# A fused linear-attention and quantized feed-forward kernel: feed-forward weights rounded by ScalarE's square, other banks for their transposes, other orders in the first and the last steps

## The reference

```
q, k = relu(x @ Wq) + 0.001, relu(x @ Wk) + 0.001        # 16 heads of 64
v = x @ Wv
context = cumsum(k (x) v); D_inv = 1 / (cumsum(k) . q)
attn = (q . context) * D_inv;  return attn @ Wo + bo

def fp4_quant_dequant(x):                                # blocks of 16 on the last axis
    scale = max(max|x| / 6, 1e-12)
    q = GRID[searchsorted(MID, |x / scale|)] * sign(x) * scale      # grid 0 .5 1 1.5 2 3 4 6
fp4_linear(x, w) = quant(x) @ quant(w).T
ffn(x) = fp4_linear(silu(fp4_linear(x, w_gate)) * fp4_linear(x, w_up), w_down)
```

## Time and profile before

| | us |
|---|---|
| median of 3 runs | 1744.37 (1743.95 to 1745.25) |
| the profiled execution | 1745.42 |
| its span, first to last instruction | 1743.4 |
| TensorE busy | 1678.0 (96%) |
| VectorE, ScalarE, GpSimd busy | 1159.6, 647.5, 454.8 |
| mean granted TensorE clock | 0.984 of full |

### The profile page before, as it was taken

One profiled execution on the slowest core, in us unless ns is written; L12 is line 12 of the kernel. 1 busy time (PEld: TensorE's weight loads), 2 busy tenths in 40 slices (PEclk: granted clock), 3 DMA queues, 4 the chain that ended last, 5 costly groups with the idle time before them and its releaser, 6 DMA issues.

```text
span 1743.4 us, 47014 instructions
## 1 busy us (share of the span) xinstructions
PE 1678.0 (96%) x20388; PEld 1590.3 (91%) x20388; DVE 1159.6 (67%) x2458; ACT 647.5 (37%) x1233; POOL 454.8 (26%) x643
## 2 busy tenths in 40 slices
PE   6679999999999999999999999999999999999985
PEld 5579999999999999999999999999999999999975
DVE  7547666766666766666676666677666667666674
ACT  5133333334333334334333433334343333343321
POOL 5342222222222222222222222122222222222211
PEclk9789999999999999999999999999999999999998
DMA  3100000000000000000000000000000000000000
GB/s 141 34 2 5 14 11 14 14 14 5 14 11 14 14 14 5 14 14 11 14 14 14 5 14 11 14 14 14 5 14 14 11 14 14 14 5 14 5 8 12
DMA packets 21963, 26.27 MB, mean 15 GB/s; under 512 B 1792, under 2 KB 20736, under 8 KB 21760
## 3 DMA queue, kind: packets, MB, share of 16 engines
q1 hardware_dynamic: 21760, 23.27, 4.2%
HBM read 14.88 MB, written 8.39 MB: 13 GB/s over the span
## 4 chain that ended last, share of the span: by engine, by line
PE 92%; DVE 4%; POOL 1%; ACT 1%; issue 1%; DMA 0%; POOLq 0%; DVEq 0%
PE bank L387 62%; PE bank L483 7%; PE bank L443 7%; PE bank L507 3%; PE bank L474 3%; PE bank L546 3%; PE bank L453 3%; PE bank L497 3%; PE bank L524 1%; PE bank L397 1%; DVE probs L1022 0%; PE bank L577 0%; DVE hid L988 0%; DVE h_amax L976 0%; DVE w_magic L944 0%
## 5 line engine op out<-in xcount | busy, mean ns | idle before, releaser
L649 ACT ACTIVATE qkT<-bank 128x512 f32<-128x512 f32 x256 | 153.4, 599 | 305.8 <-PE bank L387 305.8
L821 POOL TENSOR_SCALAR qkT<-qkT 128x512 f32<-128x512 f32 x256 | 174.9, 689 | 322.7 <-ACT qkT L649 322.7
L387 PE MATMUL bank<-xT_hi,wqk_hi 128*128 128x256 f32 x1024 | 211.8, 288 | 0.2 <-DVE wu_lo L896 0.2
L387 PE MATMUL bank<-xT_lo,wqk_hi 128*128 128x256 f32 x1024 | 203.2, 279 | 0.0
L387 PE MATMUL bank<-xT_hi,wqk_lo 128*128 128x256 f32 x1024 | 203.0, 279 | 0.0
L896 DVE TENSOR_TENSOR hqT_lo<-bank,hqT_hi 128x512 fp32r<-128x512 f32 (+1 forms) x128 | 68.3, 556 | 183.2 <-ACT hqT_hi L703 183.2
L1022 DVE TENSOR_TENSOR probs<-bank,causal 128x512 f32<-128x512 f32 x256 | 163.9, 682 | 10.9 <-PE bank L443 10.5
L850 POOL TENSOR_TENSOR rstd<-var,minus_half 128x1 f32<-128x1 f32 x64 | 35.1, 549 | 510.9 <-DVE var L1073 510.9
L387 PEld LDWEIGHTS bank<-xT_hi,wqk_hi 128*128 128x128 f32 x1024 | 155.5, 188 | 2.4 <-issue 0.3
L387 PEld LDWEIGHTS bank<-xT_lo,wqk_hi 128*128 128x128 f32 x1024 | 156.4, 188 | 0.0
L387 PEld LDWEIGHTS bank<-xT_hi,wqk_lo 128*128 128x128 f32 x1024 | 156.4, 188 | 0.0
(11 more groups left out here) (151 smaller groups left out, 3708.5 us busy)
## 6 DMA issues: line engine op xcount, KB each, us to landing
x_in<-in_L_attn_x SPq DMA_DIRECT2D x32, 256.0 KB, 2.7
out<-out_sb SPq DMA_DIRECT2D x64, 128.0 KB, 1.7
probs<-in_L_attn_Wv SPq DMA_DIRECT2D x1, 1024.0 KB, 5.0
qkT<-in_L_attn_Wq SPq DMA_DIRECT2D x1, 1024.0 KB, 7.3
qkT<-in_L_attn_Wk SPq DMA_DIRECT2D x1, 1024.0 KB, 9.3
attn<-in_L_attn_Wo SPq DMA_DIRECT2D x1, 512.0 KB, 10.2
x<-in_L_attn_Wo SPq DMA_DIRECT2D x1, 512.0 KB, 11.0
hid<-in_L_ffn_w_down SPq DMA_DIRECT2D x1, 352.0 KB, 3.0
```

The source lines that it names most:

```text
L387: at = pe.matmul(dst, lhs_at(kt), rhs_at(kt), start=first and kt == 0, stop=last and kt == k_tiles - 1)
L649: act.activation(flat(qkT[:, 2 * m:2 * m + 2, :]), bank[bank_of["qk", c, n]][:], ACT.Relu).then_inc(qk_relu, 1)
L821: pool.tensor_scalar(at, at, QK_EPS, 1.0, ALU.add, ALU.mult).then_inc(qk_ready, 1)
```

## The change

1. **Rounding of the weights.** `round_magic`, the tiles `w_magic` and GpSimd's add and subtract are gone. VectorE's `quantize` becomes `quantize_begin` and `quantize_end`, with ScalarE's `square_weights` between them, as for activations. GpSimd keeps only the multiplication by the scale (`scale_weights`).
2. **Split of the attention weights.** The high part of Wv is now a VectorE copy (ahead of ScalarE's other four), and the low parts of Wo move from GpSimd to VectorE.
3. **Banks.** A job's transposes take the bank entry of a stage that does not exist yet in that step (`W_BANKS`), and the table of places starts in step 0: no job is transposed ahead of step 0.
4. **First steps.** `quantize_begin`, `quantize_end` and the squares are put at places of their own in the orders of VectorE, ScalarE and GpSimd.
5. **Last steps.** The last two steps with attention (g = 62 and 63, `last`) do the transposes of xq and hq first, the down product before attention, and scale h one step after the other. The three draining steps have an order of their own on ScalarE (`tail`) and VectorE.

```diff
+        JOBS_AT = {(0, "attend"): (0,), (0, "update"): (1,), (0, "end"): (2,), (1, "scores"): (3,),
+                   (1, "project"): (4,), (1, "end"): (5,), (2, "scores"): (6,), (2, "attend"): (7,)}
+        W_BANKS = [("hq", 0, 0), ("hq", 0, 1), ("down", 0, 0), ("xq", 1, 0), ("gate_up", 1, 0), ("down", 1, 0),
+                   ("kv", 2, 0), ("av", 2, 3), ("hq", 2, 0), ("hq", 2, 1)]
...
-                        k = banks.take(pe, ("w", "first", m), 0, ffn_w_ready, lambda b, m=m: m + 1)
+                        k = banks.take(pe, W_BANKS[m], 0, ffn_w_ready, lambda b, m=m: m + 1)
...
+                last = now and not following
...
+                if last:
+                    turn_xq(b, c, g - 2)
+                    for n in range(2):
+                        turn_hq(b, c, g - 3, n)
                 if now:
                     scores(b, c, g, u)
...
+                if last:
+                    down(b, c, g - 3)
...
+            def square_weights(job):
+                act.wait_ge(ffn_w_step, 4 * job + 4)
+                cols = ffn_jobs[job][2]
+                act.activation(w_square[:, job % 2, 0:cols], w_stage[job % 3][:, 0:cols], ACT.Square,
+                               scale=SQUARE_SCALE).then_inc(ffn_w_square, 1)
...
-                    pool.tensor_tensor(scaled, scaled, magic, ALU.add).then_inc(ffn_w_round, 1)
-                    pool.wait_ge(ffn_w_round, 2 * job + 1)
-                    pool.tensor_tensor(scaled, scaled, magic, ALU.subtract).then_inc(ffn_w_round, 1)
...
-                if exists(g - 2, ALL_CHUNKS) and (c % 2 == 1 or g >= ALL_CHUNKS):
+                if exists(g - 2, ALL_CHUNKS) and (c % 2 == 1 or g >= ALL_CHUNKS - 2):
...
+            dve.tensor_copy(hi, src).then_inc(wv_hi_ready, 1)
+            low(lo, src, hi, wv_hi_ready, 1, attn_w_ready)
             low_x("first", 0)
...
+            def quantize_end(job):
+                cols = ffn_jobs[job][2]
+                tile, square = w_stage[job % 3][:, 0:cols], w_square[:, job % 2, 0:cols]
+                dve.wait_ge(ffn_w_square, job + 1)
+                dve.scalar_tensor_tensor(tile, square, SQUARE_SHIFT, tile, ALU.add, ALU.add).then_inc(ffn_w_grid, 1)
+                dve.wait_ge(ffn_w_grid, 2 * job + 1)
+                dve.scalar_tensor_tensor(tile, square, SQUARE_SHIFT, tile, ALU.add, ALU.subtract
+                                         ).then_inc(ffn_w_grid, 1)
...
+                    elif gated:
+                        low_xq()
+                        for half in range(2):
+                            gated_by_silu(half)
+
+                        dve.wait_ge(hq_ready, g - 2)
+                        begin_h()
+                        for n in range(2):
+                            low_hq(n)
+                        round_h(g - 2)
+                        residual()
```

More of the change, by code:

```diff
@@ L610, in step @@
                         project_qk(b, c, u + 1, 2 * n, 2 * n + 2)
-                    if downed and (now or not gated):
+                    if downed and (following or not gated):
                         turn_hq(b, c, g - 3, n)
@@ L623, in step @@
                     project_qk(b, c, u + 1, 4, PAIRS)
-                if downed:
+                if downed and not last:
                     down(b, c, g - 3)
@@ L693, in step @@
                 project = c % 2 == 1 and now and following
+                if not now:
+                    tail(b, c)
+                    return
+                last = not following
                 def high_attn(n):
@@ L733, in step @@
                         relu_qk(c, u + 1, 2 * n + 1)
-                    if downed and (now or not gated):
+                    if downed and not last:
                         high_hq(n)
+                    if g == 1 and n == 1:
+                        square_weights(6)
                 high_ffn_weights(jobs_at(g, "project"))
@@ L746, in step @@
                         high_attn(half)
-                if downed and gated and not now:
-                    for n in range(2):
-                        high_hq(n)
                 if project:
@@ L998, in low_ffn_weights @@
                         m += first_turn_of(job)
-                        low(lo[:, rows, cols], part(turn[bank_of["w", "first", m]]), hi[:, rows, cols],
+                        low(lo[:, rows, cols], part(turn[bank_of[W_BANKS[m]]]), hi[:, rows, cols],
                             ffn_w_hi, m + 1, ffn_w_ready)
@@ L1004, in _ @@
             ln1_var_of(1)
-            quantize(0)
-            quantize(1)
-            quantize(2)
-            low_ffn_weights(JOBS_AT["before"])
+            for n in (3, 4):
+                src, hi, lo = attn_weights[n]
+                low(lo, src, hi, attn_w_hi, n, wo_w_ready)
+            quantize_begin(0)
+            quantize_begin(1)
+            quantize_end(0)
+            quantize_begin(2)
+            quantize_end(1)
+            quantize_end(2)
             def step(b, c):
@@ L1059, in step, with low_xq, variance @@
                 following = exists(u + 1, ALL_HALVES)
+                last = now and not following
                 norm = c % 2 == 1 and now and exists(u + 2, ALL_HALVES)
+                def low_xq():
+                    low(flat(xqT_lo[:]), flat(turn[bank_of["xq", c, 0]][:, 0:KD, :]), flat(xqT_hi[:]),
+                        xqT_hi_ready, g - 1, xqT_ready)
+                def variance():
+                    dve.bn_aggr(mv2[:], stats2[:]).then_inc(ln2_mean, 1)
+                    dve.wait_ge(ln2_mean, g)
+                    dve.tensor_scalar(minus_mean2[:], mv2[:, 0:1], -1.0, None, ALU.mult)
+                    dve.tensor_scalar(var2[:], mv2[:, 1:2], LN_EPS, None, ALU.add).then_inc(ln2_var, 1)
@@ L1102, in step @@
                     add_state()
+                if is_step(0):
+                    quantize_end(3)
+                if is_step(1):
+                    quantize_begin(6)
                 low_ffn_weights(jobs_at(g, "update"))
-                if downed and (now or not gated):
+                if downed and not last:
                     for n in range(2):
@@ L1134, in step @@
                     ln1_var_of(u + 2)
-                if gated and (c % 2 == 1 or not now):
+                if gated and (c % 2 == 1 or last):
                     round_h(g - 2)
-                if downed:
-                    dve.wait_ge(down_done, g - 2)
-                    if g >= 5:
-                        dve.wait_ge(out_stored[c % 2], 16 * ((g - 3) // 2))
-                    dve.tensor_tensor(out_sb[:, c % 2, :], bank[bank_of["down", c, 0]][:, 0:DIM],
-                                      x2[:, (c - 3) % CHUNKS, :], ALU.add).then_inc(out_ready, 1)
+                if downed and not last:
+                    residual()
                 if now:
```

288 lines of the change are left out of this document (181 added, 107 removed).

## The result

The changed kernel takes 1718.38 us (median of 4 runs, 1716.63 to 1720.26) against 1744.31 of the kernel before on the same chip (4 runs, 1743.95 to 1745.25): a ratio of 0.9851, 95% interval 0.9834 to 0.9868. That is 25.9 us less, where 31.8 were forecast. The profiled execution of it took 1718.61, with a span of 1716.2.

What follows compares the result with a forecast made beforehand. TensorE was taken as full from 160 to 1640 us, leaving only the ends: 29.1 us gained at the front plus 2.7 at the back, 31.8 off the 1743.4 span, forecast a median of 1712.6 us, range 1703 to 1723.

Steps and rivals of the forecast that it cites:

- The full stretch: 160 to 1640 us, TensorE busy 1479.85 of 1480 us at clock 1.00: the change has nothing to win there.
- First products: Start of launch: VectorE's Wv copy takes 1.2 to 2.29 us; values start at 9.15, end at 17.4 instead of 20.08.
- Weight pieces: Weight jobs at the front: chain from begin to hq ready 5.1 us instead of 6.6; VectorE ends jobs 0 to 2 at 30.0.
- the 0.7 us that I added for two meetings: Step 0, ahead of the output projection: two VectorE instructions beside GpSimd add 0.7 us, 41.8 to 42.5.
- The two waits: TensorE waits 3.5 us at step 1's state update and 3.0 for step 2's keys, plus slow clock of 1.35 and 1.3.
- Last steps: Steps 62 to the end: 0.4 us gained by step 65's gates, 2.3 at the end, 2.7 in all.
- 3.5 late in all: By step 63, hq's transposes ahead of the scores and other new waits put TensorE 3.5 us behind the old order.
- C: Rival: the 3.5 us lost by step 63 are not won back, VectorE's queue only moving waits: 1718.8 us; chance 0.14.
- B: Rival: more waiting at the front, from VectorE contending with GpSimd, step 2 and a slow clock: 1722 us; chance 0.12.
- A: Rival: VectorE is 3 us faster, so the new front waits and their slow clock (9.2 us) go: 1703.4; chance 0.14.
- D: Rival: slower, because the long stretch loses its full clock or its order's fit; chance 0.03.
- E: Rival: nothing happens, since the jobs' real limit is their loads: 1744 us; chance 0.02.

Runs made afterwards that it cites:

- wv_scalar: The changed kernel with Wv's high-part copy back on ScalarE ahead of its other copies, VectorE only subtracting: 1720.01 us.
- k_first: The changed kernel with ScalarE's copies of the transposed keys ahead of the normalization of x2 in step 2 alone: 1713.74 us.
- old_places: The changed kernel with its new rounding, but the weight jobs at the places and in the banks of the kernel before: 1731.67 us.
- drain_only: The changed kernel with steps 62 and 63 in the order of before, new orders kept for draining steps 64 and 65: 1710.73 us.

## Why the prediction was right, and where it was off

**Where the time is.** Right in the main. The full stretch bounded the kernel, and all but 2.1 us of the gain came from the 11 us wait, the slow clock behind it and the first products.

**The number.** In the spans 27.2 us were gained where 31.8 were forecast: 3.4 too few at the front, 3.3 too few at the back, and 2.1 in the middle that nobody had counted on. That the total is off by 4.6 and not by 6.7 is luck.

**First products.** The copy took 1.23 us, near its lower bound of 1.2, so the values started at 9.22 and did not wait. (The Trainium skill, VectorE: DVE Perf Modes, "Mode 2×_2P", says that a float32 copy within SBUF makes two results a cycle; the trace agrees, 1.23 for 2048 columns against 2.29 for the subtraction.) The projections ended at 27.9 instead of 28.7. How much of these 3 us reaches the end of the sum, wv_scalar leaves open, between 1.6 and 4.

**Weight pieces.** The step that failed at the front is "products that lay beside GpSimd's work ... mostly lie alone", with the 0.7 us that I added for two meetings. VectorE ended jobs 0 to 2 at 32.3, not 30.0: up to there six instructions stood behind GpSimd's, for 0.30, 0.41, 0.74, 0.41, 0.41 and 0.96 us, 3.2 in all, and later 0.74 at 41.76, 0.37 at 53.39, 0.87 at 70.30 and 1.07 at 81.39. The last of these also held the low part of job 5, which the key transposes of step 2 waited for.

**Steps 0 to 2.** Output projection of step 0 ended 46.8 (forecast 45.35), state update of step 1 began 60.5 (59.05), that of step 2 97.3 (93.9). The two waits have the causes that were forecast and nearly the sizes, and k_first confirms the second, slow clock included. Of the 3.4 us that are missing, 1.45 are there by the end of step 0, ahead of both waits, where the meetings of the last paragraph lie. The other 1.9 arise between the two state updates: a wait of 0.58 at 73.64 for a low part of w_up, behind the meeting at 70.30; 0.5 in the wait for k_tok; and the price of the slow clock, put at 1.35 and 1.3. By the windows it was 1.7 each time (0.73, 0.50 and 0.91 in the 2 us windows from 60 to 66; 0.56 and 0.59 from 88 to 92). No run took the meetings away, so their share is argued from the timelines.

**Last steps.** The forecast gain of 2.7 is not there, and by its own sign, a back longer than before, the prediction was wrong here. "3.5 late in all" by the end of step 63 was 6.2; the draining steps' 6.2 were 5.6 in this execution, and up to 7.8 in others with the same orders. The single waits were well forecast (3.87 for 3.65, 1.48 for 1.35, 1.12 for 1.15). What failed is that the sum priced no slow clock behind 5.4 us of idle time in step 63 (and took off about 0.5 for the one of before), although it did so for every wait at the front: the scores alone lost 1.73 us, the down product behind them about 0.5. The wait of 2.27 at the gate of step 65 was not seen at all; I had the residual put ahead of h's rounding and did not ask what stood behind the rounding. The last scaling came 5.9 us behind the last product, as forecast.

**The full stretch.** "The change has nothing to win there" was wrong by 2.1 us, for a reason that no view of the profile of before could show.

**What made the gain.** Of 25.9 us the places make 13 to 16 (old_places), the banks nothing, the Wv copy 1.6 to 4, where the tiles lie 1.8 to 2.5, the last steps nothing. The rest, some 3 to 10, falls to the shorter rounding with Wo's move; that is by subtraction and was not run alone. The prediction did not separate places from banks.

**Rivals.** C (the last steps cost) gave 1718.8, and 1718.4 was measured, but that is chance. It had a loss of 3.5 us and no gain behind it, because VectorE's queue only moves the waits; there were a loss of 6.2 and a gain of 5.6, and drain_only shows that the waits are not just moved. B's contention is what happened at the front. A, D and E did not occur.

## What to carry to other kernels

Do not move work that must wait ahead of work that is free to run: the new order of steps 62 and 63, with hq's transposes ahead of the scores, cost 6 to 8 us, and the waits of 3.71, 3.47 and 3.87 us in the changed kernel were each paid a second time in the slow clock behind them. Where two in-order engines hold each other up, put the instructions that meet apart, and count a meeting as the rest of the other's instruction, not as a factor. When an edit has several halves, measure them apart: here the sum of zero hid one half worth 8 us and another that cost as much.

## What the runs showed of the hardware

**VectorE beside GpSimd is a stop, not a slow-down.** In the changed kernel's trace 30 of the 66 small instructions that make h_scale (0.186 us alone, one source, in SBUF) start while a GpSimd instruction runs; all of these take the rest of GpSimd's plus their own 0.186 less 0.146 to 0.148. GpSimd stands likewise: its scaling at 80.58, which began beside VectorE's rounding at 80.42, took 2.02 us, the next one of the same size at 89.44 took 1.39. Not touched are reductions (0.68 at 25.15, beside a GpSimd instruction), reciprocals (0.35 at 26.82, likewise) and subtractions with a source in PSUM (0.68 at 43.11, beside the addition at 42.60). Nor was a subtraction of two sources in SBUF at 18.11 beside GpSimd's power over two columns; that power, begun at 17.15 beside the subtraction before it, itself took 1.61 where it took 0.71 at 5.11. The Trainium skill (SBUF — State Buffer, "Who interferes with whom") says it of one shared pair of ports: an exclusive lock, which whoever starts first keeps for the whole instruction. Apart from 18.11 the trace agrees. I had priced a meeting by one row of before (1.28 for 0.69), 0.59; it can be the whole of GpSimd's instruction.

**Where tiles lie in SBUF moved TensorE's pace** by 0.07 us in 30.56, as shown above. No other number of the profile shows it: the granted clock is 1.00 and there is no idle time in either.
